# Four stacked triangle layers on one core: another path for the transposed activation, fewer and moved passes, and clock products between layers

## What is computed

```python
x = x + L0(gn(x));  x = x + L1(gn(x));  x = x + L2(gn(x));  x = x + L3(gn(x))
# inside a layer (l = 0; the others differ in biases, masks and orientation)
xn    = layernorm(x)                       # layer 3: no layer norm on its input
left  = (xn @ Wl) * mask * sigmoid(xn @ Wlg)
right = (xn @ Wr) * mask * sigmoid(xn @ Wrg)
gate  = sigmoid(xn @ Wog)
t     = einsum('bikd,bjkd->bijd', left, right)   # for each channel a 192x192x192 product
out   = (layernorm(t) * gate) @ Wout             # layers 1 and 3: (layernorm(t) @ Wout) * gate
```

## Time and profile before

| | us |
|---|---|
| median of 3 runs (1522.71 to 1531.39) | 1524.15 |
| profiled execution | 1531.67 |
| its span | 1529.5 |

### The profile page before, as it was taken

One profiled execution on the slowest core, in us unless ns is written; L12 is line 12 of the kernel. 1 busy time (PEld: TensorE's weight loads), 2 busy tenths in 40 slices (PEclk: granted clock), 3 DMA queues, 4 the chain that ended last, 5 costly groups with the idle time before them and its releaser, 6 DMA issues. The chain is left out here.

```text
span 1529.5 us, 43851 instructions
## 1 busy us (share of the span) xinstructions
PE 1282.1 (84%) x12950; PEld 765.9 (50%) x12950; DVE 1041.8 (68%) x2976; ACT 962.0 (63%) x2093; POOL 543.4 (36%) x490
## 2 busy tenths in 40 slices
PE   0899998787789998989941999999789677799898
PEld 0455554444345455755521666667455333367455
DVE  7577774299789996219950788831499788821587
ACT  0577774489577774129940888831599688822575
POOL 0455551055456563005530666610156200000355
PEclk9899999899899999999975899999899899999999
DMA  8011113467533332896667333359689444369798
GB/s 275 27 52 46 51 51 111 114 202 225 169 101 103 106 115 72 254 286 177 195 152 188 103 115 113 108 174 300 180 262 278 154 141 138 129 185 307 212 291 258
DMA packets 206501, 249.31 MB, mean 163 GB/s; under 512 B 29024, under 2 KB 196320, under 8 KB 206432
## 3 DMA queue, kind: packets, MB, share of 16 engines
q1 hardware_dynamic: 206432, 248.42, 53.1%
HBM read 139.83 MB, written 108.53 MB: 162 GB/s over the span
## 5 line engine op out<-in xcount | busy, mean ns | idle before, releaser
L989 DVE SCALAR_TENSOR_TENSOR lr<-ps,mask,act_out 128x128 f32 (+5 forms) x1152 | 276.3, 310 | 61.7 <-ACT act_out L739 55.6
L1153 POOL TENSOR_TENSOR rstd<-ve,half_col 128x6 f32<-128x6 f32 x144 | 190.2, 1321 | 259.1 <-DVE ve L962 225.4
L511 PE MATMUL ps<-w_parts,val 64*128 64x256 bf16 (+1 forms) x2112 | 222.6, 304 | 47.4 <-DVE lr L989 41.9
L1196 POOL TENSOR_TENSOR new_ring<-val,lr 128x384 f32<-128x384 f32 x96 | 103.4, 1078 | 409.5 <-issue 325.0
L1186 POOL TENSOR_TENSOR val<-act_out,gate_ring 128x384 f32<-128x384 f32 x96 | 118.4, 1233 | 247.2 <-ACT act_out L817 231.1
L739 ACT ACTIVATE act_out<-ps 128x384 f32<-128x384 f32 x384 | 174.9, 481 | 34.2 <-PE ps L511 16.7
L783 ACT ACTIVATE in_ring<-ps 128x768 f32<-128x768 f32 (+1 forms) x64 | 51.8, 810 | 184.0 <-PE ps L579 161.9
L511 PEld LDWEIGHTS ps<-w_parts,val 64*128 64x128 bf16 (+1 forms) x2112 | 90.5, 111 | 133.3 <-DVE lr L989 94.7
L1085 DVE TENSOR_TENSOR sq_low<-sq 128x384 bf16<-128x384 f32 x192 | 120.1, 625 | 52.9 <-ACT sq L796 52.8
L621 PE MATMUL ps<-in_ring,k 128*128 128x384 f32 x288 | 134.5, 555 | 20.1 <-DMA in_ring<-t_scratch 19.7
L715 ACT ACTIVATE cen<-ps,gn 128x384 f32<-128x384 f32 x144 | 83.6, 581 | 104.1 <-PE ps L466 101.5
(11 more groups left out here) (101 smaller groups left out, 2574.8 us busy)
## 6 DMA issues: line engine op xcount, KB each, us to landing
gate_scratch<-gate_ring SPq DMA_DIRECT2D x192, 192.0 KB, 2.2
gate_ring<-gate_scratch SPq DMA_DIRECT2D x96, 384.0 KB, 3.7
in_ring<-x_scratch SPq DMA_DIRECT2D x144, 192.0 KB, 2.4
lr<-x_scratch SPq DMA_DIRECT2D x72, 384.0 KB, 4.5
in_ring<-t_scratch SPq DMA_DIRECT2D x144, 192.0 KB, 3.3
x_scratch<-new_ring SPq DMA_DIRECT2D x48, 384.0 KB, 2.9
t_scratch<-in_ring SPq DMA_DIRECT2D x48, 384.0 KB, 3.4
lr<-x SPq DMA_DIRECT2D x6, 1536.0 KB, 15.3
```

The lines of the kernel that those rows point to most:

```text
L511: mm = nc.tensor.matmul(banks[h][:, :, 0:P], moving(x, s)[half(h), N * r:N * r + P], proj_weights(w, h)[:, 0:2 * P], start=start, stop=sto ...
L989: ins = nc.vector.scalar_tensor_tensor(out5[:, h, lo // 2:hi // 2, :, m], ps[:, 4 + 2 * r + h, lo:hi].rearrange("p (a e) -> p a e", e=2), ...
L1153: nc.gpsimd.tensor_tensor(rstd[:, s % 2, :], ve[:, s % 2, :], half_col[:, :], ALU.pow)\
```

## The change

Eight edits:

1. The turned x is stored to a new DRAM array in the layout in which it lies in `lr`: SP stores the first 8 rows of each half (two DMAs), ScalarE's own queue the other 88 (two DMAs).
2. Stage A of layer 2 gathers a pair of tiles at once from it (`gather`, two DMAs with runs of 96 elements) and stores each pair back to `x_scratch` in natural order (`keep`), from where stage B1 loads the residual.
3. Halved instructions for layer 2 are gone (`column_parts`, `x_parts`). VectorE's wait for the turned store now stands behind the first four tiles' preparation.
4. Layer 3, stage A: the high part is no copy but the upper halves of xn's words, read in place (`xn_high`); ScalarE's order is changed (`plain` behind the sigmoids).
5. Layer 0, stage B2: no square_low; the variance is taken by f32 products.
6. Stage B1: from group 14 on, residual loads are issued after the first t loads of stage B2 (`late_loaded`); the first two gate loads of stage B2 are issued at group 12.
7. Start of stage B2: centrings and small products in another order; one call of keep_clock instead of three inside it.
8. `group_norm` of layers 1 to 3: keep_clock calls (2, 1, 1) before the three small products.

```diff
-EARLY = 8
+EARLY = 4
+LATE = 14
+    turned_dram = nc.dram_tensor("turned_scratch", [2, 2, C, HALF, HALF], F32).ap()
+        xn_high = xn[...].bitcast(BF16).rearrange("p s (f e) -> p s f e", e=2)[:, :, :, 1]
+        def turned_rows(h2, first, behind):
+            return (turned_dram[:, h2, :, first:behind, :],
+                    turned[:, HALF * h2 + first:HALF * h2 + behind, :])
...
 # SP, phase_a
+                def gather(n, s):
+                    for h in range(2):
+                        rows = turned_dram[h].rearrange("h2 c j i -> (h2 c) j i")[:, bass.ds(ROWS * n, 2 * ROWS), :]
+                        slot = in_ring[:, s:s + 2, :].rearrange("p a (r i) -> p (a r) i", r=ROWS)
+                        sp.dma_start(slot[:, :, HALF * h:HALF * h + HALF], rows).then_inc(in_loaded[s], 16)
+                def keep(n, i, s):
+                    sp.wait_ge(in_loaded[s], in_count(l) + 32 * (i + 1))
+                    sp.dma_start(two_tiles(scratch, n), in_ring[:, s:s + 2, :]).then_inc(natural_stored[s // 2], 16)
+                def step_gathering(n, i, s, ahead):
+                    if s % 2 and ahead >= RING + lead - 1:
+                        sp.wait_ge(used, l * TILES + n + lead + 1)
+                        sp.wait_ge(natural_stored[s // 2], 16 * (i + 2))
+                        gather(n + lead + RING - 1, s - 1)
+                    sp.wait_ge(a_gate, l * TILES + n + 1)
+                    sp.dma_start(gate_dram[n, :, :], gate_ring[:, s, :]).then_inc(gate_stored[s], 16)
+                    if s % 2 and ahead >= RING + 1:
+                        keep(n + RING + 1, i + (s + 5) // RING, (s + 1) % RING)
+                if l == 2:
+                    gather(0, 0); gather(2, 2); keep(0, 0, 0); keep(2, 0, 2)   # loops in the source
+                    sp.wait_ge(turned_stored[1], 16 * 2)
+                    ...                        # gather 4 and 6 once tiles 1 and 3 are used and kept
+                    keep(RING, 1, 0)
+                    over_tiles(sp, step_gathering, 2 * RING)
...
 # SP, phase_b1 and phase_b2
-                    for n in freed_slots(l, g) if l else []:
+                    for n in freed_slots(l, g) if l and g < LATE else []:
+                        load_residual(l, n, res_loaded)
+                    if g == LATE - 2:
+                        ...                    # wait for gate_stored
+                        for n in range(0, RING, 2):
+                            load_gate(l, n, n)
                 for n in range(0, RING, 2):
                     load_t(n, n)
-                    load_gate(n, n)
+                for g in range(LATE, GROUPS) if l else []:
+                    for n in freed_slots(l, g):
+                        load_residual(l, n, late_loaded)
...
-                    for part, tiles in enumerate((slice(0, EARLY), slice(EARLY, TILES))):
-                        ...                    # 2 x 4 stores, 64 partitions each
-                    sp.wait_ge(turned_stored[0], 16 * 4)
+                    for h2 in range(2):
+                        sp.dma_start(*turned_rows(h2, 0, ROWS * EARLY)).then_inc(turned_stored[0], 16)
+                    sp.wait_ge(turned_stored[0], 16 * 2)
...
 # TensorE, group_norm
+                if l:
+                    ...                        # wait for tile 46's finish
+                    keep_clock(4, 2)
                 pe.wait_ge(gn_dve, 7 * l + 1)
                 nc.tensor.matmul(ps[:, 6, 0:1], k_group, mv[:, 0:1], ...)
+                if l:
+                    keep_clock(4, 1)
                 ...                            # second product, keep_clock(4, 1) again, third
 # TensorE, phase_b2
+                    if l == 0:
+                        pe.wait_ge(b2_sq, base + n + 1)
+                        for j in range(CHUNKS):
+                            mm = nc.tensor.matmul(ps[:, 6 + s % 2, 2 * j:2 * j + 2],
+                                                  sq[:, s % 2, P * j:P * j + P], k_sel, start=True, stop=True)
-                for n in range(4):
-                    centre(n, 0, n)
+                centre(0, 0, 0)
+                centre(1, 0, 1)
                 keep_clock(4, 1)
                 variance(0, 0)
-                keep_clock(4, 1)
+                centre(2, 0, 2)
                 ...                            # centre 3 and 4 between the spreads, no third keep_clock
 # ScalarE
-                    if not ln and ahead >= 1:
-                        high(n + 1, (s + 1) % RING)
-                    if not ln and ahead >= 2:
-                        plain(n + 2, ...)      # now behind both sigmoids
+                    act.wait_ge(b2_turned, TILES)
+                    for h2 in range(2):
+                        act.dma_start(*turned_rows(h2, ROWS * EARLY, HALF)).then_inc(turned_stored[1], 16)
 # VectorE
+                        nc.vector.tensor_tensor(xn_parts[:, s % 2, 1, :], xn[:, s % 2, :], xn_high[:, s % 2, :],
+                                                ALU.subtract).then_inc(a_lo, 1)
-                        for new, out, x in zip(column_parts(l, new_ring[:, s, :]), ...):
-                            ins = nc.vector.scalar_tensor_tensor(new, out, bias, x, ALU.add, ALU.add)
+                        nc.vector.scalar_tensor_tensor(new_ring[:, s, :], ps[:, 4 + s % 2, 0:TILE], bias, residual_slot(l, n),
+                                                       ALU.add, ALU.add).then_inc(b2_new, 1)
-                    if ahead >= 4:
+                    if l and ahead >= 4:
                         square_low(n + 4, s)
```

More of the change, by code:

```diff
@@ L217, in freed_slots, with residual_count @@
             return [n for n in pairs if n < TILES]
+        def residual_count(l, late):
+            return 16 * sum(len(freed_slots(m, g)) for m in range(1, l + 1) for g in range(GROUPS) if (g >= LATE) == late)
         def two_tiles(dram, n):
@@ L313, in step @@
                     sp.dma_start(gate_dram[n, :, :], gate_ring[:, s, :]).then_inc(gate_stored[s], 16)
+                if l == 2:
+                    for n in range(0, RING, 2):
+                        gather(n, n)
+                    for n in range(0, RING, 2):
+                        keep(n, 0, n)
+                    sp.wait_ge(turned_stored[1], 16 * 2)
+                    for n in range(0, RING, 2):
+                        sp.wait_ge(used, l * TILES + n + 2)
+                        sp.wait_ge(natural_stored[n // 2], 16)
+                        gather(RING + n, n)
+                    keep(RING, 1, 0)
+                    over_tiles(sp, step_gathering, 2 * RING)
+                    return
                 if l:
@@ L342, in phase_b2 @@
                     sp.wait_ge(planes_stored[s], (l + 1) * 48 * (GROUPS // 2))
-                for s in range(RING):
-                    sp.wait_ge(gate_stored[s], (l + 1) * 16 * TURNS)
                 def load_t(n, s):
@@ L389, in phase_b2 @@
                     sp.wait_ge(b2_turned, TILES)
-                    quarters = scratch.rearrange("t (h2 c) (h f) -> h h2 c t f", h2=2, h=2)
-                    for part, tiles in enumerate((slice(0, EARLY), slice(EARLY, TILES))):
-                        for h in range(2):
-                            for h2 in range(2):
-                                rows = turned[C * h:C * h + C, h2 * HALF:(h2 + 1) * HALF, :]
-                                sp.dma_start(quarters[h, h2, :, tiles, :],
-                                             rows.rearrange("p (t r) i -> p t (r i)", r=ROWS)[:, tiles, :])\
-                                    .then_inc(turned_stored[part], 16)
-                    sp.wait_ge(turned_stored[0], 16 * 4)
+                    for h2 in range(2):
+                        sp.dma_start(*turned_rows(h2, 0, ROWS * EARLY)).then_inc(turned_stored[0], 16)
+                    sp.wait_ge(turned_stored[0], 16 * 2)
                 else:
@@ L447, in moving @@
                 def moving(part, s):
+                    if not ln and part == 0:
+                        return xn_high[:, s % 2, :]
                     return xn_parts[:, s % 2, part, :] if IN_PARTS[l] else val[:, s % 2, :]
@@ L463, in centre @@
                     slot_free(pe, a_ve, base + n - 1)
[L464 to L467 removed]
+                    nc.tensor.matmul(ps[:, s % 2, 0:TILE], w_centre[:, :], in_ring[:, s, :] if l else x_all[:, n, :],
+                                     start=True, stop=True).then_inc(a_z, 1)
                 def variance(n, s):
@@ L555, in phase_a @@
                 over_tiles(pe, step)
-            def keep_clock(bank, count):
-                for _ in range(count):
-                    nc.tensor.matmul(ps[:, bank, 0:TILE], k_centre, k[:, 0:TILE], start=True, stop=True)
             def phase_b1(l):
@@ L761, in step @@
                         centred(n + 4, s)
+                    if not ln and ahead >= 2:
+                        plain(n + 2, i + (s + 2) // RING, (s + 2) % RING)
                 if ln:
@@ L770, in phase_a @@
                     plain(0, 0, 0)
```

(10 more changed lines are left out.)

96 lines of the change are left out of this document (55 added, 41 removed).

## The result

The changed kernel takes 1629.95 us (median of 4 runs, 1622.65 to 1635.43) against 1525.41 (4 runs) for the kernel before: ratio 1.0677, 95% interval 1.0623 to 1.073. It is slower by about 104 us where 60 less were forecast. The profiled execution of after took 1635.43 us, its span is 1633.2.

What follows compares the result with a forecast made beforehand. Bounds by stage: DMA alone at the seam, VectorE in layers 0 and 2's output stages, ScalarE and VectorE in layer 3's input, TensorE in layer 2's. -24-13-7-5-9-2 = -60 from 1524.15 gives 1464 us; range 1450 to 1478.

Steps and rivals of the forecast that it cites:

- Seam: Between layers 1 and 2: faster turned store, prologue hidden behind it; -24 us, ends -8 and -31.
- the store is no faster: Seam: store stays at 216 GB/s because memory, not runs, is the bound; 1480 us, chance 0.08.
- the first gathers wait for the long rows: Seam: first gathers land only when the store does, prologue follows; 1474 us, chance 0.10.
- the gathers come late: Layer 2's input stage: gathers exceed their 10 us; 1542 us at 16.5 us per gather, chance 0.04.
- Layer 3's stage A: Input stage: without ScalarE's bf16 copy, 2.52 us per tile; -13 us, ends -18 and -4.
- Layer 0's stage B2: Output stage: no square_low, f32 variance on TensorE, 2.02 us per tile; -7 us, ends -9 and +10.
- TensorE takes over: Layers 0 and 3: f32 variance costs 0.19 per pass, high part streams at half rate; 1490 us, chance 0.12.
- Layer 2's stage B2: Output stage: one residual instruction replaces two halves; -5 us, ends -6 and 0.
- Starts of stage B2: Output stage starts: moved loads, fewer clock products and interleaved order; -9 us, ends -14 and 0.
- Fillers: Group norm: clock-keeping calls speed the third small product and first tiles; -2 us, ends -6 and +3.

Runs made afterwards that it cites:

- full-height run: Changed kernel with the DRAM scratch laid out so each turned store covers 128 partitions, its slowest dimension 128, and four gathers per pair of tiles: 1482.96 us.
- the twelve runs above: Twelve follow-up kernels varying the turned store, gate and residual loads, fillers, square_low, or layer 3's copy and order: medians from 1476.22 to 1631.84 us.
- the fastest kernel here: Changed kernel with full-height stores of 128 partitions, 1.5 KB runs, and first gate loads back at the start of stage B2: 1476.22 us.

## Why the prediction was wrong, and where it was right

**Seam: -24 forecast, +129 measured. This is the failed step.** It took "one run per row" and "every DMA covers 128 partitions" and gave the store 325 GB/s by the row of the x load. The second half is true of the SBUF side; nothing in the step asked how many engines the DRAM side allows. Two engines moved 54 GB/s, and T, the end of the whole store, came 177 us after the issue, not 34. A rule of the Trainium skill says so: "DMA: Bandwidth & Descriptors", section "Why a DMA increments its semaphore by 16 and not by 1", lets the slowest dimension above size 1 of both access patterns set the engines, the largest number up to 16 that divides both. By that, [2, 64, ...] gives 2, and 64 or 128 gives 16; the packet counts 4, 64 and 32 above agree. The prediction cites two other sections of that page.

With 16 engines and full height the step comes close: from bn_aggr to the first gate 60.6 us in before, 38.6 in that run, 22 less. That is in part luck, since two misses cancel: the rate was better than my upper end, 431 GB/s against 370, while the prologue of four tiles, which I had hidden behind the store, came after it (first centring 27.5 us after the issue of a store that ends after 23.6). The full height that the prediction names is needed too: sixteen engines at half height give only 1.3 us less (55.5 to 54.2). (The fast end of -31 should read -29 by its own working: 30 us of store, then 6.5 and 1.5.)

**Rival "the store is no faster".** Its rate came true for stores of 64 partitions (220 GB/s, long runs or short), its reason, the memory, did not: 431 GB/s go to the same memory. The share of 0.93 in the earlier trace rows that I used for it speaks neither way, since it is 0.98 at 220 and 1.01 at 431. The Trainium skill, "SBUF — State Buffer", section "Door 1: The DMA port swizzle", gives the reason, which no run here isolates: 64 partitions of one half reach 8 of 16 ports, 218 GB/s against 436.

**Rival "the first gathers wait for the long rows"** (0.10) is true in every run with 34 KB runs: the early part is complete after 159.8, 40.6 and 21.6 us, near the end of the store, although it went by another queue. The packets of the trace show how. In after 30 early packets go first; from then on the two engines take one early packet (3 KB, 0.12 us) and one late packet (34 KB, 1.25 us) in turn, so that 226 of the 256 late packets have started before the last early one. In the runs with 16 engines and long runs it is 223 to 227 of 256. So the packet-wise turns of which the prediction spoke are there. With 1.5 KB runs the early part takes 14.0 us at half height and 7.1 at full height, but the first gathers then run beside the store and need 15.7 and 11.1 us from issue to the first centring, against 5.9 in the full-height run with long runs. I had put this rival too low.

**Rival "the gathers come late":** no. Layer 2's gates take 158.7 us against 159.5 in before, gathers land in 2.7 us.

**Layer 3's stage A:** -12.2 against -13. The pace is 119.63 / 47 = 2.55 us against 2.52 taken. VectorE is busy 103.8 of 110 us, as expected. TensorE did not stream the high part at half rate: the gate's passes that read it in place took 337 ns, the packed one 324. (That end of the range was also worked out wrongly: 0.32 us x 47 tiles is 15 us, which leaves nothing of the 13 and not 4.)

**Layer 0's stage B2:** -11.3 against -7. The pace is 91.75 / 47 = 1.95 us where I took 2.02, so ScalarE's 1.97 was the better guess. The six passes of a tile took 0.58 us (353.26 to 353.84), 0.10 each where I took 0.12, so TensorE's tile is a little shorter than forecast. It stands at 84.4 of 85 us all the same: "TensorE takes over" was close to true, at ScalarE's pace. (The sum's end of +10 should read +13: 2.44 - 2.17 = 0.27, x 47.) Putting square_low back cost 9.8 us of the stage but only 5.7 between the medians (7.0 by the two ratios to before); in that profile layer 2's output stage is 4.3 us shorter than in its base, which the edit doesn't touch, and why is open.

**Layer 2's stage B2:** -3.4 in after, -4.5 to -9.6 in the twelve runs above, against -5. One instruction for two saves VectorE 5.6 us (34.6 - 29.0). No run puts the halves back, and the stage takes anything from 94 to 100 us in kernels that do not differ in it, so this term is of the right size but not shown.

**Starts of stage B2:** -9 forecast, +4.3 measured for B1 and start together: the starts alone (last plane copy to first Wout product) are 3.2 us shorter, the stretches in front of them (last gate to last plane copy) 7.5 longer. With the gate loads put back the two together are -6.9. I priced the gate loads at nothing where they had been moved to, in the stage B1 that waits for its own stores, and the starts too high.

**Fillers:** -2 forecast, about -1 in the stretches, nothing that the times show.

**Sum.** The forecast was 60 less. With the engine count and the height of the stores put right, the full-height run's median is 1482.96 us against 1523.99 for before beside it, 41 less, and the fastest kernel here is 48 less. (The profiled executions of the full-height run and of before, 1477.1 and 1531.7, are 55 apart, but the first is the fastest of its four runs and the second slower than the four of before that the result rests on.) Runs of one kernel lie up to 10 us apart here, and the sum is confirmed no closer than that.

## What to carry to other kernels

Before you price a large DMA, write down the slowest dimension of both its sides: it sets the engines, and a slice such as `x[:, h]` of a small outer axis can leave two of them. Then ask how many partitions the SBUF side spans: 64 ran at half the rate of 128, with the same busy share. If anything small must pass while a big store runs, give the big store short runs; another queue alone did not help, since the packets of the two queues took turns one for one. But price the whole store as well: with short runs it ended 7 us later here, and the stage waits for its end.

## What the runs showed of the hardware that was not expected

- One DMA engine moved about 27 GB/s (54 by two, 431 by sixteen), with runs of 34 KB.
- Stores of 64 partitions on all engines: 220 to 222 GB/s, in two DRAM layouts; of 128 partitions: 431 GB/s. The busy share was 0.98 to 1.01 in all.
- Gathers in 384 B runs landed in 2.5 to 2.7 us (medians) and stage A of layer 2 did not feel the extra 9.4 MB (158.7 against 159.5 us). A 384 B packet took 0.023 to 0.026 us, which is 15 to 17 GB/s an engine against 27 with 34 KB.
- A packet of 34 KB took 1.2 to 1.3 us, and 2.4 at half height. Two queues took turns packet by packet, 3 KB against 34 KB: a store of 0.79 MB in one finished only when 223 to 227 of the 256 long packets in the other had started.
